# Node scores as two columns of the linear stage, and the row order found in the convolution's node stage

## The reference

```
def _L1_gnn_ref(x, edge_index, W_w, W_b, a_w, a_b):
    h = x @ W_w + W_b
    row, col = (edge_index[0], edge_index[1])
    a_src, a_dst = (a_w[:DIM], a_w[DIM:])
    e = h[row] @ a_src + h[col] @ a_dst + a_b
    e = jax.nn.leaky_relu(e, negative_slope=0.01)
    attention = jax.nn.softmax(e, axis=0)
    msg = attention * h[col]
    out = jax.ops.segment_sum(msg, row, num_segments=N_NODES)
```

## Time and profile before

| what | value |
|---|---|
| time, median of 3 runs | 5465.58 us (5462.35 to 5475.82) |
| the profiled execution: time, span | 5463.36 us, 5461.6 us |
| PE busy | 3942.8 us (72%) |
| DVE busy | 3383.7 us (62%) |
| POOL busy | 3245.9 us (59%) |
| ACT busy | 1286.2 us (24%) |

### The profile page before, as it was taken

One profiled execution on the slowest core, in us unless ns is written; L12 is line 12 of the kernel. 1 busy time (PEld: TensorE's weight loads), 2 busy tenths in 40 slices (PEclk: granted clock), 3 DMA queues, 4 the chain that ended last, 5 costly groups with the idle time before them and its releaser, 6 DMA issues. The chain is left out here.

```text
span 5461.6 us, 98938 instructions
## 1 busy us (share of the span) xinstructions
PE 3942.8 (72%) x21586; PEld 3392.6 (62%) x21587; DVE 3383.7 (62%) x8848; ACT 1286.2 (24%) x2426; POOL 3245.9 (59%) x3303
## 2 busy tenths in 40 slices
PE   4655665535999999957775666666654999999987
PEld 3555555524888888846664555555543777777765
DVE  6555555575433433347777677777777677777666
ACT  1111111112333333346663111111104222222211
POOL 4777777713777777730000777777760777777760
PEclk7777677655666656567777566666667999999998
DMA  5666666612333333334441444444432666666651
GB/s 140 154 156 155 156 157 156 145 19 61 102 106 102 102 104 104 102 92 112 112 111 54 130 128 129 128 128 129 127 102 79 188 180 178 180 179 178 179 166 40
DMA packets 640707, 689.16 MB, mean 126 GB/s; under 512 B 96871, under 2 KB 506427, under 8 KB 640478
## 3 DMA queue, kind: packets, MB, share of 16 engines
q0 software_dynamic: 132032, 325.99, 22.0%
q1 hardware_dynamic: 398750, 306.82, 20.8%
q10 hardware_dynamic: 109824, 55.39, 3.6%
HBM read 553.47 MB, written 134.38 MB: 126 GB/s over the span
## 5 line engine op out<-in xcount | busy, mean ns | idle before, releaser
L1326 POOL DMA_INDIRECT R<-table_kv,h_idx x832 | 812.3, 976 | 878.4 <-DVE h_idx L1379 625.6
L1515 POOL DMA_INDIRECT X<-table_ps,r_idx x832 | 814.1, 978 | 413.0 <-issue 228.0
L1140 POOL DMA_INDIRECT by_src<-R,p_idx x832 | 814.5, 979 | 317.1 <-issue 223.5
L625 POOL DMA_INDIRECT R<-table,c_idx x784 | 761.1, 971 | 268.2 <-issue 227.7
L1353 PE MATMUL psum<-R,h_oh 128*128 128x137 f32 x1664 | 374.2, 390 | 398.8 <-DVE R L1433 395.2
L656 PE MATMUL psum<-R,c_oh 128*128 x1664 | 345.9, 373 | 420.2 <-ACT R L666 252.2
L1353 PEld LDWEIGHTS psum<-R,h_oh 128*128 128x128 f32 x1664 | 315.4, 272 | 442.1 <-DVE R L1433 433.3
L656 PEld LDWEIGHTS psum<-R,c_oh 128*128 128x128 f32 x1664 | 294.2, 266 | 469.6 <-issue 469.6
L1532 PE MATMUL psum<-w_L_gnn_re_w,r_ea 128*128 128x256 f32 x1664 | 506.2, 386 | 81.0 <-DVE early_cols L1576 79.6
L996 PE MATMUL psum<-src_score,R 128*128 128x50 f32 x1664 | 439.3, 356 | 31.5 <-issue 22.7
L1234 PE MATMUL psum<-R 128*128 128x128 f32 x1664 | 351.0, 377 | 147.1 <-DVE R L1248 144.8
(11 more groups left out here) (316 smaller groups left out, 7494.7 us busy)
## 6 DMA issues: line engine op xcount, KB each, us to landing
by_src<-fill ACTq DMA_DIRECT2D x208, 260.0 KB
R<-by_src SPq DMA_DIRECT2D x208, 260.0 KB
r_ea<-in_ea_t SPq DMA_DIRECT2D x832, 64.0 KB
R<-in_ea_t SPq DMA_DIRECT2D x196, 256.0 KB
R<-rel_rows SPq DMA_DIRECT2D x104, 256.0 KB
R<-lo_rows SPq DMA_DIRECT2D x104, 256.0 KB
h_rel<-rel_rows SPq DMA_DIRECT2D x208, 128.0 KB
r_rel<-rel_rows SPq DMA_DIRECT2D x208, 128.0 KB, 3.3
```

What stands on the lines that cost most here:

```text
L625: g.indirect_dma_start(out=rows[:, u, :], out_offset=None, in_=table, in_offset=bass.IndirectOffsetOnAxis(ap=idx[:, j // GROUPS % 2, u:u + ...
L1140: g.indirect_dma_start(out=by_src, out_offset=bass.IndirectOffsetOnAxis(ap=idx[:, u:u + 1], axis=0), in_=rows[:, u, :], in_offset=None).th ...
L1326: g.indirect_dma_start(out=rows[:, u, :], out_offset=None, in_=table, in_offset=bass.IndirectOffsetOnAxis(ap=idx[:, u:u + 1], axis=0)).the ...
L1515: g.indirect_dma_start(out=rows[:, u, :], out_offset=None, in_=table, in_offset=bass.IndirectOffsetOnAxis(ap=idx[:, u:u + 1], axis=0)).the ...
```

## The change

Two stages are gone as stages.

The scores: `W` and its bias get two more columns each, `W @ a_src`, `W @ a_dst` and `b . a_src`, `b . a_dst`, made once at the end of `phase_tables` by four multiplications with a sum per partition (`W` lies with its rows on the partitions, so a sum along a row times `a_w` gives the entry of the new column). `phase_linear` then writes rows of 130, and the last two entries are the scores. `fit` becomes 3, so a group of 4 tiles leaves PSUM in two instructions (3 tiles and 1). `phase_permute` copies the source scores to a small tile, and reads the others in place.

The order: the body of `phase_order` moves, as class `Order`, into `phase_conv_nodes`, ahead of what VectorE and TensorE do there; SP's part runs beside. It uses PSUM bank 2 and the free buffer R3.

```diff
@@ phase_tables, VectorE, last instructions
+                for side in range(2):
+                    a_w = k.b["L1_gnn_a_w"][:, side * D:(side + 1) * D]
+                    for wide_row in (k.w_scored, k.b_scored):
+                        link(v.scalar_tensor_tensor(out=junk[:, 0:D], in0=wide_row[:, 0:D], scalar=1.0, in1=a_w, op0=ALU.mult,
+                                                    op1=ALU.mult, accum_out=wide_row[:, D + side:D + side + 1]))
@@ phase_linear
-        banks = (3, 5, 7) if cols > P else (3, 4, 5)
+        banks = (3, 5, 7) if fit < 4 else (3, 4, 5)
@@ new
+class Order:
...
+    def tensor(self, pe):
+        pe.wait_ge(self.cast, 1)
...
+        mm.then_inc(self.summed, 1)
+    def vector(self, link, v):
+        link(v.memset(self.nought, 0.0))
+        v.tensor_copy(self.count16[:], k.count[:, :, 0:NT]).then_inc(self.cast, 1)
+        v.wait_ge(self.summed, 1)
...
+        v.tensor_copy(self.digit[:], self.part_i).then_inc(self.digits_known, 1)
+        for j in range(SB):
+            link(v.tensor_scalar(self.junk[:, 0:RT], self.upto[:, 0:RT], k.step_no[:, j:j + 1], 0.0, ALU.is_le, ALU.add,
+                                 accum_out=self.node[:, j:j + 1]))
+        v.tensor_copy(self.table, self.node).then_inc(self.table_known, 1)
+    def sync(self, sp):
+        sp.wait_ge(self.digits_known, 1)
...
+        sp.dma_start(k.order[0:1, :], k.order_dram[0:1, :]).then_inc(self.got, 16)
+        sp.wait_ge(self.got, 16)
+        sp.wait_ge(self.stored, 48)
@@ phase_conv_nodes
             @block.vector
             def _(v):
                 link = vector_chain(chain, v)
+                order.vector(link, v)
                 for n, cut in enumerate(norm.CUTS):
                     v.wait_ge(activated, n + 1)
...
+            @block.sync
+            def _(sp):
+                order.sync(sp)
...
             def _(pe):
+                order.tensor(pe)
                 for n in range(2):
                     pe.wait_ge(want, n + 1)
@@ phase_scores_nodes and phase_order: removed
@@ phase_permute
-                        pe.matmul(cols[:, 0:NT], is_lo[:, j, q * P:(q + 1) * P], k.src_score[:], start=True, stop=True)
+                        pe.matmul(cols[:, 0:NT], is_lo[:, j, q * P:(q + 1) * P], src_score[:], start=True, stop=True)
...
-                                       k.dst_score[:, bass.ds(regs["node"][G8 * j + q], 1), :], start=True, stop=True)
+                                       H[:, bass.ds(regs["node"][G8 * j + q], 1), D + 1:D + 2], start=True, stop=True)
...
+                link(v.tensor_copy(src_score[:], H[:, :, D]))
@@ build
-        phase_linear(nc, k, "l1", k.X[:], k.w["L1_gnn_W_w"][:], D, k.b["L1_gnn_W_b"][:], half3(0))
...
-            phase_scores_nodes(nc, k, half3(0), half1(0), half1(1))
-            phase_order(nc, k, r1)
-            phase_permute(nc, k, half3(0), scores, by_src, r1, R3[:, 2 * NT * D + 2 * ST:])
+        Hx = r3[:, 0:NT * (D + 2)].rearrange("p (t d) -> p t d", d=D + 2)
+        phase_linear(nc, k, "l1", k.X[:], k.w_scored[:], D + 2, k.b_scored[:], Hx)
+        scores = r3[:, NT * (D + 2):][:, 0:ST]
+        phase_permute(nc, k, Hx, scores, by_src, r1, R3[:, 2 * NT * (D + 2) + 2 * ST:])
```

More of the change, by code:

```diff
@@ L753, in phase_conv_nodes @@
         norm = Norm(nc, c, sem, "n0_")
+        order = Order(nc, k, c, sem, room)
         total = sb("total", [P, 2, D], F32)
@@ L817, in _ @@
                     pe.matmul(k.psum[:, n, 0:D], k.ones[:], total[:, n, :], start=True, stop=True).then_inc(have, 1)
[L821 to L839, removed]
@@ L842, in phase_order @@
[L842 to L887, removed]
-                link(v.tensor_tensor_scan(upto, tiles_f, nought, 0.0, ALU.add, ALU.add))
-                link(v.tensor_tensor(first, upto, tiles_f, ALU.subtract))
-                link(v.scalar_tensor_tensor(out=base, in0=first.unsqueeze(1).to_broadcast([P, SB, NT]), scalar=float(P),
-                                            in1=k.psum[:, 0, 0:SB * NT].rearrange("p (j h) -> p j h", h=NT),
-                                            op0=ALU.mult, op1=ALU.add))
-                link(v.tensor_copy(base_i, base.rearrange("p j h -> p (j h)")))
-                link(v.tensor_scalar(part_i[:, 0, :], base_i, 12, None, ALU.arith_shift_right))
-                link(v.tensor_scalar(part_i[:, 1, :], base_i, 6, 63, ALU.arith_shift_right, ALU.bitwise_and))
-                link(v.tensor_scalar(part_i[:, 2, :], base_i, 63, None, ALU.bitwise_and))
-                v.tensor_copy(digit[:], part_i).then_inc(digits_known, 1)
-                for j in range(SB):
-                    link(v.tensor_scalar(junk[:, 0:RT], upto[:, 0:RT], k.step_no[:, j:j + 1], 0.0, ALU.is_le, ALU.add,
-                                         accum_out=node[:, j:j + 1]))
-                v.tensor_copy(table, node).then_inc(table_known, 1)
-            @block.sync
-            def _(sp):
-                sp.wait_ge(digits_known, 1)
-                for n in range(3):
-                    sp.dma_start(k.digit_dram[n].rearrange("(j p) h -> p j h", p=P),
-                                 digit[:, n, :].rearrange("p (j h) -> p j h", h=NT)).then_inc(stored, 16)
-                sp.wait_ge(table_known, 1)
-                with nc.allow_non_contiguous_dma(reason="a column per block of steps"):
-                    sp.dma_start(k.order_dram[0].rearrange("(j p) -> p j", p=P), table).then_inc(kept, 16)
-                sp.wait_ge(kept, 16)
-                sp.dma_start(k.order[0:1, :], k.order_dram[0:1, :]).then_inc(got, 16)
-                sp.wait_ge(got, 16)
-                sp.wait_ge(stored, 48)
@@ L1006, in expand @@
                             mm = pe.matmul(k.psum[:, 4 + 2 * j + h, (q % G) * D:(q % G + 1) * D],
[L1007 removed]
+                                           is_rel[:, j, q * P:(q + 1) * P], H[:, bass.ds(regs["node"][G8 * j + q], 1), 0:D],
                                            start=True, stop=True)
@@ L1838, in build @@
         k.one_eps = sb("one_eps", [P, 1], F32)
-        k.w = {n: sb("w_" + n, [P, ap[n].shape[0] // P * ap[n].shape[1]], F32) for n in RESIDENT}
+        k.w_scored, k.b_scored = sb("w_scored", [P, D + 2], F32), sb("b_scored", [P, D + 2], F32)
+        k.w = {n: sb("w_" + n, [P, ap[n].shape[0] // P * ap[n].shape[1]], F32) for n in RESIDENT if n != "L1_gnn_W_w"}
+        k.w["L1_gnn_W_w"] = k.w_scored[:, 0:D]
         k.kv = sb("w_kv", [P, 2 * D], F32)
-        k.b = {n: sb("b_" + n, [P, ap[n].shape[1]], F32) for n in ROWS_RESIDENT}
+        k.b = {n: sb("b_" + n, [P, ap[n].shape[1]], F32) for n in ROWS_RESIDENT if n != "L1_gnn_W_b"}
+        k.b["L1_gnn_W_b"] = k.b_scored[:, 0:D]
         k.kv_b = sb("b_kv", [P, 2 * D], F32)
```

62 lines of the change are left out of this document (53 added, 9 removed).

## The result

| kernel | time, median (lowest to highest) | profiled execution: time, span |
|---|---|---|
| before, 4 runs | 5470.7 us (5462.35 to 5475.86) | 5463.36, 5461.6 us |
| after, 4 runs | 5405.57 us (5398.96 to 5410.09) | 5403.79, 5402.0 us |

The ratio is 0.9882, with an interval of 0.9866 to 0.9898: 65.1 us less, between 56 and 73. The time lies in the range given, 5402 to 5428. So there are two questions: whether the five terms of the sum are right, and where the rest comes from.

The account below looks back on a forecast made before the run. It took the removed stages as bound by lone VectorE work and a DRAM round trip, the permuting loop as paced by GpSimd. -60.1 + 5.9 + 1.2 + 1.6 + 0 = -51.4 us from 5465.58 gave 5414, range 5402 to 5428.

Parts of the forecast that it names:

- Two stages removed, -60.1: Between linear stage and permuting loop: VectorE's first loop instruction moves from 1294.51 to 1234.45, 60.06 us less.
- The chain in the node stage, +5.9: Node stage: the order's chain starts with ScalarE and delays the additions of X by 5.94 us; bounds 4.7 to 7.
- Two columns, +1.2: Linear stage: ten additions of 4 tiles split in two for 130 columns cost 1.2 us, bounds 0 to 2.6.
- End of the tables, +1.6: End of the tables: four linked multiplications with a sum, some 0.4 us each, cost 1.6 us; bounds 0 and 2.2.
- Start of the permuting loop, 0: Permuting loop's start: the copy of 50 columns hides under ScalarE's wait for the `lo` row; nothing, at most 0.3 us.
- The odd price: Scores' stage: VectorE's multiplication by a_w took 20.32 us, read as waiting out GpSimd's 13.65; by lone instruction, sum about -38.
- Clock rival: Permuting loop's start: TensorE's clock stays up over the shorter gap, first half turn up to 5 us shorter, 5409; chance 0.05.
- TensorE as the bound: Permuting loop: TensorE's half turns of 11.31 us exceed GpSimd's 10.27, making it slower, up to 5522 us; chance 0.03.
- Operands' new places: Permuting loop: H's 520-byte rows and buffers moved by 400 bytes lose 10 to 35 us, 5425 to 5450; chance 0.07.
- Does less than it says: Barrier behind the linear stage costs more than its 0.79 us; 5416 to 5425; chance 0.02.
- the last step: Whole kernel: the sum of -51.4 us applied to the median of before, 5465.58, gives 5414 us.

Follow-up runs that it names:

- scores_only: The changed kernel with the row order as its own stage again between linear stage and permuting loop; 5436.44 us, 0.9933 of before.
- order_only: The kernel before with the row order moved into the node stage, the scores left as their own stage; 5454.1 us, ratio 0.9966.
- vector_scores: The kernel before with the multiplication by a_w that GpSimd did given to VectorE; 5461.81 us, ratio 0.9986.
- pad_only: The kernel before with 64 unused bytes of SBUF per partition ahead of the large buffers; 5474.82 us, ratio 1.0.
- before_again: The kernel before, unchanged, run once more; 5468.06 us, ratio 0.9997.
- after_again: The changed kernel, run once more; 5410.53 us, 0.9885 of before.
- chain_split2: The changed kernel with the order's chain on VectorE in pieces, scan and subtraction ahead of the first addition of X; 5406.57 us, 0.9879 of before.
- early_order: The changed kernel with the order as a stage of its own ahead of the node stage; 5428.87 us in one run.

## Why the prediction came out as it did

Term by term, from the rows shown:

- *Two stages removed, -60.1:* -59.6. Where 0.79 us was to stay, 1.28 stayed. In `scores_only`, where the order's stage follows the linear one, it is 0.83: it depends on the stage that follows, and the prediction took the 0.79 that stood ahead of another stage.
- *The chain in the node stage, +5.9:* the first addition of X starts 5.9 us later, the stage is 90.6 us long instead of 84.6. The choice in it, that the chain starts with ScalarE, is shown to 0.06 us. `order_only` measured this term and the order's removal together, 184.9 - 167.5 = 17.4 us in the region; by the sum it was to be 18.9.
- *Two columns, +1.2:* 22.6 us from the stage's first instruction to its last addition before, 23.6 after: +1.0.
- *End of the tables, +1.6:* 4 x 0.33 = 1.3.
- *Start of the permuting loop, 0:* 17.1 us from VectorE's first instruction to GpSimd's first transfer, 17.3 before.

Together -59.6 + 6.0 + 1.0 + 1.3 - 0.2 = -51.5, where -51.4 was forecast. The mechanism and its five sizes stand.

The odd price, 20.32 us, was where "the saving hangs on it". `vector_scores` settles it: with GpSimd beside it the multiplication took 13.5 us more, and priced by the lone instruction the saving would have come out too small by that. The Trainium skill (SBUF — State Buffer, Who interferes with whom) has a VectorE instruction with two SBUF inputs contend with a GpSimd one that reads SBUF, whichever comes first holding the port for its whole length; the traces agree, 20.32 against 6.83 us and 2.46 against 0.26.

*Clock rival:* it did not occur. The granted clock fell within 1240 to 1244, as it had within 1235 to 1239, and the first scores ran at 0.50. What a first half turn at the full clock would have given, no run shows. *TensorE as the bound:* not seen. What GpSimd waited for after, 1275 to 2370 us:
```profile
POOL by_src L1132 <- ACT R L1027: 24.7, 81, 0.3
```
That answers to the earlier trace rows; the one longer wait, 1.3 us, is in the first turn. First to last transfer is 1068.2 us against 1067.0. *Operands' new places:* nothing, by `pad_only` for the shift of the large buffers by 64 bytes, and for H's rows of 130 by the products that read them. The 400 bytes by which the loop's own buffers move have no run of their own; the loop's 1068.2 us has them in it. These are the loop's expansions after, and below them before (columns: busy, mean ns):
```profile
L997 PE MATMUL psum<-R 128*128 x1649 | 376.5, 421 | 0.0
```
```profile
L1006 PE MATMUL psum<-R 128*128 x1649 | 377.9, 422 | 0.0
```
*Does less than it says:* the barrier cost 0.5 us more, below the 2 us at which that rival began.

What failed is the last step, "against the median, 5465.58, it is 5414". It takes the rest of the program as the same, and the base as known to 2 us. Between the two profiled executions the time fell by 5463.36 - 5403.79 = 59.6: 51.5 in the terms, 2.7 in the attention ring, 3.2 in the loops, and 2.2 in what lies between. The profile of before was itself a quick execution, 7 us under the median of 5470.7, and by `before_again` such a difference lies in the loops (4243.5 against 4255.5). The 2.2 us are no gain of the change either: 3.1 of them lie between the head loop and the relation loop, 160.8 us before, 157.7 after, and 160.9 again in `after_again`. With the mean of the two executions of each kernel the spans are 62.8 us apart, where the medians give 65.1 and 63.1: 51.9 in the terms, 3.0 in the ring, 7.9 in the loops and nothing in what lies between. That is an estimate from two executions of each.

So the sum explains some 51 of 63 to 65 us, and that the time fell into the range was in part luck. The base was the median of three executions, 5465.58; with a fourth it is 5470.7. From that base the same sum gives 5419 and a range as wide lies at 5407 to 5433, which 5405.57 is outside of. The low base took back 5 of the 14 us by which the saving was too small.

Why the changed kernel's loops lie at the low end is open. Seen over the table, what the median gives beyond the terms goes with the loops of the profiled execution: 10 to 14 us more in the kernels with loops of 4240 to 4244 (`after`, `after_again`, `chain_split2`, `early_order`), 0 to 7 in those with 4246 to 4256. For the three kernels with one run this is no evidence, since their time is that of the profiled execution. The others point to a pace of its own in each kernel, but one and the same kernel shows both ends, and only before and after have a trace of a second execution. The 3 us of the ring are open too: neither the order's stage nor its DMAs separate the six executions with 474.5 to 475.1 us from the eight with 477.0 to 478.3, and for what does separate them, the chain in one piece in the node stage, there is no mechanism.

## What to carry to other kernels

When a stage between barriers has one engine busy for a quarter of it and a round trip to DRAM at its end, put its work into a stage that has an idle engine and a long way to go: what remains of it is what stands ahead of the first instruction that others wait for (5.9 of 24.8 us), and that is read from the timeline at the new place, not from the busy shares. Price a removed stage by its own stretch and not by the usual durations of its instructions, and look for GpSimd and VectorE both reading two SBUF operands. Before trusting a forecast to under 0.3%, take two profiles of the same kernel: the unchanged stages moved by 12 us here, more than all errors of the sum.

## What the runs showed that I had not expected

- GpSimd's help cost more than it saved: half of the multiplication given to it made the stage 6.6 us longer, and a scan of 50 columns took 2.46 instead of 0.26 us.
- The indirect transfers of the edge loop, which no kernel changes, took 967 to 977 ns on the mean, depending on the execution, and 971 and 977 in the two of one kernel.
- A stage that nothing touched took either 475 or 478 us, the first only where the order's chain stood whole in the node stage, by a cause that isn't found.
- At a barrier 0.79 to 1.70 us passed between the last work and VectorE's first instruction, and the same place went from 0.79 to 1.28 when another stage came behind it.
